# Cross-attention adjacency and a mixture of experts on one core: idle products by a new constant, new orders, and another last step

## The reference

```
# stage 1, for each of 4 batches (4 heads are summed, so Q K^T is one 512x512 product)
sim    = ctx Wq^T (ctx Wk^T)^T * scale           # 512 x 512
A      = sigmoid(sim) where sim is among the 153 largest of its row, else 0
A      = (A + A^T) / 2
x      = x + tanh(g_xattn) * ((1 - gamma) * layernorm(x) + gamma * A)
# stage 2, for each of 2048 tokens
n      = layernorm(x)
best 2 of 8 experts by softmax(n gate_w), their shares normed, times alpha
y_e    = gelu(n fc1[e] + b1[e]) fc2[e] + b2[e]    # 512 -> 512 -> 512
x      = x + tanh(g_ffn) * sum over the two experts of share * y_e
```

## Time and profile before

| what | value |
|---|---|
| median of 3 runs | 366.69 us |
| lowest, highest | 365.43, 367.62 us |
| the profiled execution | 365.13 us |
| its span on the core | 363.4 us |
| mean granted TensorE clock | 0.958 |
| busy PE, PEld | 324.3 us (89%), 232.9 us (64%) |
| busy DVE, ACT, POOL | 200.7 us (55%), 165.0 us (45%), 100.1 us (28%) |
| DMA | 65.79 MB, mean 181 GB/s |

### The profile page before, as it was taken

How to read it: one execution, slowest core, us unless ns; L and a number is a source line. 1 busy time by engine, 2 the same in 40 slices (tenths; PEclk the granted TensorE clock), 3 DMA queues, 4 the chain that set the end, 5 groups by cost and what they waited for, 6 DMA issues and landing times.

```text
span 363.4 us, 6131 instructions
## 1 busy us (share of the span) xinstructions
PE 324.3 (89%) x1937; PEld 232.9 (64%) x1937; DVE 200.7 (55%) x697; ACT 165.0 (45%) x384; POOL 100.1 (28%) x141
## 2 busy tenths in 40 slices
PE   6906899779998999899999989999999999999960
PEld 4402667677764786678778576777785877577610
DVE  0488698887879777898886372636206112311010
ACT  2485515389996746256786222232222213132320
POOL 5001001361111357114307431331733111312031
PEclk9975699899999999999999999999999999999996
DMA  2999989977974696876627587744678854533253
GB/s 91 379 392 369 352 298 331 378 267 139 305 145 123 144 243 231 146 161 183 113 54 181 191 173 135 211 100 81 203 163 149 176 119 104 111 64 87 30 74 46
DMA packets 53636, 65.79 MB, mean 181 GB/s; under 512 B 9792, under 2 KB 28512, under 8 KB 53600
## 3 DMA queue, kind: packets, MB, share of 16 engines
q1 hardware_dynamic: 46144, 47.99, 43.7%
q0 software_dynamic: 7456, 17.37, 24.7%
HBM read 39.56 MB, written 25.78 MB: 180 GB/s over the span
## 4 chain that ended last, share of the span: by engine, by line
PE 50%; issue 18%; DVE 14%; DVEq 5%; DMA 5%; POOL 3%; POOLq 2%; ACT 2%; ACTq 0%
PE ps L1711 21%; PE ps L1684 13%; PE ps L1694 10%; DMA out_rows<-ab,dst 3%; PE ps L1647 2%; POOL xs_rows L566 2%; DMA meta<-xs_rows 2%; DVE top L1087 1%; DVE stats L1012 1%; PE ps L1607 1%; PE ps L1721 1%; PE ps L1627 1%; PE ps L1639 1%; POOLq L530 1%; DVEq L1086 1%
## 5 line engine op out<-in xcount | busy, mean ns | idle before, releaser
L1684 PEld LDWEIGHTS ps<-xgT_r,weights 128*128 128x128 f32 x768 | 87.8, 192 | 8.3 <-issue 6.7
L1684 PE MATMUL ps<-xgT_r,weights 128*128 128x128 f32 x768 | 89.6, 276 | 3.6 <-ACT xgT_r L743 2.0
L1711 PE MATMUL ps<-weights,act_r 128*128 128x512 f32 x192 | 86.3, 595 | 1.5 <-ACT act_r L766 1.5
L580 POOL DMA_INDIRECT out_rows<-ys,dst x24 | 37.9, 1578 | 115.2 <-ACT ys L773 70.0
L1711 PEld LDWEIGHTS ps<-weights,act_r 128*128 128x128 f32 x192 | 34.9, 190 | 38.4 <-issue 36.5
L766 ACT ACTIVATE act_r<-ps,b1T 128x128 f32<-128x128 f32 x96 | 27.1, 365 | 38.9 <-PE ps L1684 38.8
L1694 PEld LDWEIGHTS ps<-sim,weights 128*128 128x128 f32 x256 | 35.2, 190 | 1.9 <-issue 1.7
L566 POOL DMA_INDIRECT xs_rows<-ab,pos x32 | 31.9, 998 | 14.5 <-issue 9.1
L1694 PE MATMUL ps<-sim,weights 128*128 128x160 f32 x256 | 35.6, 299 | 0.0
L773 ACT ACTIVATE ys<-ys,meta 128x512 f32<-128x512 f32 x24 | 17.3, 719 | 31.3 <-DVE ys L1322 31.3
L1322 DVE TENSOR_TENSOR ys<-ps,b_r 128x512 f32<-128x512 f32 x24 | 16.5, 686 | 23.4 <-PE ps L1711 22.0
(11 more groups left out here) (206 smaller groups left out, 419.0 us busy)
## 6 DMA issues: line engine op xcount, KB each, us to landing
weights<-in_L_ffn_fc_w SPq DMA_DIRECT2D x16, 1024.0 KB, 8.0
b_r<-in_L_ffn_fc_b SPq DMA_DIRECT2D x32, 256.0 KB, 4.1
xg_r<-xs_rows SPq DMA_DIRECT2D x88, 64.0 KB
xb<-in_x SPq DMA_DIRECT2D x4, 1024.0 KB, 7.1
out_rows<-xb SPq DMA_DIRECT2D x4, 1024.0 KB, 5.5
sim<-xs_rows SPq DMA_DIRECT2D x32, 80.0 KB
xs_rows<-weights SPq DMA_DIRECT2D x1, 2064.0 KB, 13.5
xs_rows<-weights SPq DMA_DIRECT2D x2, 516.0 KB, 5.9
```

Source lines behind the costliest of these rows:

```text
L580: pool.indirect_dma_start(out=out_rows, out_offset=bass.IndirectOffsetOnAxis(ap=dst[:, k % 2, e:e + 1], axis=0), in_=result_rows(m), in_of ...
L1684: mm = pe.matmul(ps[:, n % 2, i * P:(i + 1) * P], weights[:, e, 0, h, i * P:(i + 1) * P], rows[:, h * P:(h + 1) * P], start=(h == 0), stop ...
L1711: mm = pe.matmul(ps[:, 2 + m % 2, :], rows, weights[:, e, 1, i, :], start=(i == 0), stop=(i == IB - 1))
```

## The change

The idle products read a new constant `warm`, which VectorE fills with ones. TensorE waits for it with `warm_ok` instead of for `consts`, runs 36 idle products instead of 24, and gets two further groups of 8, ahead of `project(0)` and ahead of the first scores. The fill is the first statement of VectorE's list; the wait at the top of VectorE's program (line 978) is untouched and comes before it.

The last part is changed. `tails(1)` comes ahead of expert 7's second layer and takes its number, 32; expert 7's result is now number 33 (`LAST_NO`). Expert 7's second layer is split into two halves around `hand_over` and `merge(1)`. `hand_over` is one product more: a third matrix of zeros and ones picks from the weighed tails those rows whose token is also in expert 7's tile, and brings them to that token's row there. `find_twins` adds up which tail rows were handed over, and these too are pointed at thrown-away rows. So expert 7's tile and the tails have no token in common, and `add_result(3, 7)` no longer waits until the tails have been added: it waits for the add before them. Bias and share of expert 7's tile are applied by two operations of VectorE (`open_last`, `close_last`) in place of `add_bias` and `weigh`.

The lists of all five engines are rearranged. The first part of TensorE's, and the parts of the other lists of which the text speaks, are shown; "..." marks what is left out.

```
-BUSY_LOADS, BUSY_SEARCH, BUSY_MASK = 24, 36, 48
+BUSY_LOADS, BUSY_SEARCH, BUSY_MASK = 36, 36, 48
...
+        warm = sb("warm", [P, P], BF16)
...
+        LAST_NO = FULL + E + GROUPS - 1
+
         def result_no(k, e):
-            return k * E + e if k < BATCH - 1 else FULL + (SHARE + 1) * (e // SHARE) + e % SHARE
+            if k < BATCH - 1:
+                return k * E + e
+            return LAST_NO if e == E - 1 else FULL + (SHARE + 1) * (e // SHARE) + e % SHARE
...
@@ SyncE's list
             store_x1(0)
-            fill_pads()
-            load_weights(6)
             load_x(2)
-            load_weights(7)
             load_meta(0)
             load_rows(0, 2)
             load_rows(0, 3)
+            fill_pads()
             fill_ends()
...
             load_rows(0, 6)
             load_b2(0, 4)
+            load_weights(6)
+            load_rows(0, 7)
             store_x1(1)
             load_b2(0, 5)
-            load_rows(0, 7)
+            load_weights(7)
...
@@ GpSimd, add_result
-                pool.wait_ge(ys_ok, m + 1)
-                if m:
-                    pool.wait_ge(added, 16 * m)
+                if m == LAST_NO:
+                    pool.wait_ge(twins_ok, 1)
+                    pool.wait_ge(last_ok, 1)
+                    pool.wait_ge(added, 16 * (m - 1))
                 else:
-                    pool.wait_ge(pad_out, 32)
+                    pool.wait_ge(ys_ok, m + 1)
...
@@ GpSimd's list
+            scatter_rows(3, 0)
+            scatter_rows(3, 1)
             add_result(2, 3)
-            for t in range(BT):
-                scatter_rows(3, t)
+            scatter_rows(3, 2)
             add_result(2, 4)
+            scatter_rows(3, 3)
             add_result(2, 5)
...
             add_result(3, 6)
+            add_tails(1)
             add_result(3, 7)
-            add_tails(1)
...
@@ ScalarE's list (new order around the first gelu)
             norm_plain(0)
             norm_plain(1)
-            norm_plain(2)
-            norm_plain(3)
             scores(2, 0)
             scores(2, 1)
             leaning(0)
+            norm_plain(2)
+            context(3)
+            norm_plain(3)
+            picked(0)
             scores(2, 2)
             scores(2, 3)
...
+            signs(1, 0)
             query(3)
-            signs(1, 0)
-            picked(0)
             picked(1)
             signs(1, 1)
             gelu(0, 0)
...
@@ VectorE
+            def open_last():
+                u = LAST_NO % 2
+                dve.wait_ge(handed_ps, 1)
+                dve.wait_ge(b2_in_s[u], b2_count(LAST_NO))
+                dve.wait_ge(added, freed(LAST_NO))
+                dve.scalar_tensor_tensor(result_rows(LAST_NO), b2_r[:, u, :], last_share, ps[:, SMALL_BANK, :], ALU.mult,
+                                         ALU.add)
+
+            def close_last():
+                u = LAST_NO % 2
+                dve.drain()
+                dve.wait_ge(y_ps, LAST_NO + 1)
+                dve.scalar_tensor_tensor(result_rows(LAST_NO), ps[:, 2 + u, :], last_share, result_rows(LAST_NO), ALU.mult,
+                                         ALU.add).then_inc(last_ok, 1)
...
@@ VectorE's list
+            dve.memset(warm[:], 1.0).then_inc(warm_ok, 1)
             coefficients()
             x_stats(0, 0)
-            for t in range(BT):
-                sim_stats(0, t)
+            sim_stats(0, 0)
+            x_stats(0, 1)
+            sim_stats(0, 1)
+            sim_stats(0, 2)
+            sim_stats(0, 3)
             first_guess(0)
-            keep_gate_sum()
+            x_stats(0, 2)
             count(0, 0)
-            x_stats(0, 1)
             narrow(0, 0)
             count(0, 1)
-            x_stats(0, 2)
+            x_stats(0, 3)
             narrow(0, 1)
             count(0, 2)
-            x_stats(0, 3)
             x_var(0)
             narrow(0, 2)
+            x_stats(1, 0)
             x_scales(0)
-            x_stats(1, 0)
+            keep_gate_sum()
...
             best_two(0)
+            gaps(0)
             norm(0, 2)
             norm(0, 3)
-            x_var(1)
-            sim_stats(1, 0)
-            gaps(0)
-            sim_stats(1, 1)
             one_hot(0)
             shares(0)
+            places(0)
+            sim_stats(1, 3)
             one_hot(1)
...
@@ TensorE
-                        pe.matmul(ps[:, 3, 0:P], ones_b[:], ones_b[:], start=True, stop=True)
+                        pe.matmul(ps[:, 3, 0:P], warm[:], warm[:], start=True, stop=True)
...
+            def hand_over():
+                pe.wait_ge(tails_w, GROUPS)
+                pe.wait_ge(twins_ok, 1)
+                pe.matmul(ps[:, SMALL_BANK, :], twins[:, GROUPS, :], result_rows(tail_no_of(GROUPS - 1)), start=True,
+                          stop=True).then_inc(handed_ps, 1)
...
@@ TensorE's list
+            pe.wait_ge(warm_ok, 1)
+            keep_busy(BUSY_LOADS)
             pe.wait_ge(consts, 2)
-            keep_busy(BUSY_LOADS)
             pe.wait_ge(qk_in, 32)
             pe.matmul(ps[:, 0, 0:C], wq, wk, start=True, stop=True).then_inc(m_ps, 1)
             turn_context(0)
             pe.wait_ge(m_sb, 1)
+            keep_busy(8)
             project(0)
+            keep_busy(8)
             for t in range(BT):
                 scores(0, t)
+            turn_context(1)
+            project(1)
+            scores(1, 0)
+            scores(1, 1)
             turn_b1()
             sum_gate()
-            turn_context(1)
-            project(1)
+            busy_to_threshold()
+            prove(0)
             turn_context(2)
-            scores(1, 0)
-            scores(1, 1)
-            busy_to_threshold()
             scores(1, 2)
-            prove(0)
             scores(1, 3)
             keep_busy(BUSY_MASK)
...
-            scores(2, 0)
-            scores(2, 1)
+            for t in range(3):
+                scores(2, t)
+            rank(0)
+            scores(2, 3)
             keep_busy(12)
-            rank(0)
-            scores(2, 2)
-            scores(2, 3)
+            project(3)
             pick_rows(0)
-            project(3)
             pick_rows(1)
             layer1(0, 0)
             layer1(0, 1)
             layer2(0, 0)
+            layer2(0, 1)
             layer1(0, 2)
-            layer2(0, 1)
...
+            layer1(1, 7)
             layer2(1, 6)
-            layer1(1, 7)
+            layer2(1, 7)
             adjacency(3, 0)
             adjacency(3, 1)
             layer1(2, 0)
-            layer2(1, 7)
...
             layer2(3, 6)
-            layer2(3, 7)
             tails(1)
+            layer2(3, 7, 0, 2)
+            hand_over()
             merge(1)
+            layer2(3, 7, 2, 4)
```

More of the change, by code:

```diff
@@ L846, in _ @@
                 halve(1, t)
-            weigh(0, 1)
-            gelu(0, 3)
+            signs(2, 0)
             gelu(0, 4)
-            signs(2, 2)
-            for t in range(BT):
-                affine_x(2, t)
+            affine_x(1, 3)
+            signs(2, 1)
             weigh(0, 2)
             turned(1, 0)
+            weigh(0, 3)
             turned(1, 1)
-            weigh(0, 3)
             turned(1, 2)
             turned(1, 3)
-            candidates(2, 0)
-            candidates(2, 1)
+            leaning(1)
@@ L861, in _ @@
             scores(3, 0)
-            candidates(2, 2)
+            gelu(0, 5)
+            signs(2, 2)
+            weigh(0, 4)
+            for t in range(3):
+                candidates(2, t)
+            gelu(0, 6)
+            affine_x(2, 0)
+            candidates(2, 3)
+            squash(2, 0)
             scores(3, 1)
-            candidates(2, 3)
+            weigh(0, 5)
+            affine_x(2, 1)
+            squash(2, 1)
+            gelu(0, 7)
             scores(3, 2)
-            leaning(1)
@@ L894, in _ @@
-            weigh(1, 2)
-            turned(2, 3)
-            for t in range(BT):
-                candidates(3, t)
-            gelu(1, 3)
-            squash(3, 0)
+            turned(2, 3)
+            candidates(3, 1)
+            squash(3, 0)
+            candidates(3, 2)
+            candidates(3, 3)
+            weigh(1, 2)
+            gelu(1, 4)
+            weigh(1, 3)
             squash(3, 1)
+            leaning(2)
+            gelu(1, 5)
+            squash(3, 2)
+            squash(3, 3)
@@ L1358, in _ @@
                 total(0, t)
-            for t in range(BT):
-                add(0, t)
+            add(0, 0)
+            add(0, 1)
+            x_stats(1, 1)
+            add(0, 2)
+            add(0, 3)
             for t in range(BT):
@@ L1464, in _ @@
-            add(2, 3)
-            for t in range(BT):
-                x1_stats(2, t)
-            x1_var_of(2)
-            narrow(3, 1)
-            norm_bias(2)
-            for t in range(BT):
-                norm(2, t)
-            turn_rows(1, 4)
-            add_bias(10)
-            narrow(3, 2)
-            x_scales(3)
-            largest(3, 0)
+            add_bias(10)
```

(16 more changed lines are left out.)

493 lines of the change are left out of this document (268 added, 225 removed).

## The result

The changed kernel takes 379.99 us (median of 3 runs, 378.96 to 380.74), against 366.69 us before. The ratio is 1.0363, interval 1.03 to 1.0427: 13.3 us slower, where 3.4 us faster was forecast. The profiled execution took 378.96 us with a span of 377.1 us, 13.7 us more than the 363.4 of before.

A forecast was written before the change was run, and what follows sets the result against it. Bounds: batch 0's chain before 66.8 us, three engines near their limit to 114, TensorE's own work to 346.8, then a 16.6 us tail. Sum -0.2 + 0 - 3.2 = -3.4 us, so 363.3 us, range 359.9 to 368.2.

The forecast's parts named there:

- The dense stage: TensorE from 114 to 346.8 us: a 1.2 us gain set against new waits, 0 us, bounds -3.0 and +3.0.
- The prediction's own sign of being wrong: Wrong if TensorE waits more than 4 us between batch 1's transposes and the last layer.
- The first idle products: Program start: fill at 9.34 us, products near 9.6, joined matrix at 13.7, 8.7 us later than before.
- the rival had 8.7: Program start: products run from the first microsecond, the 8.7 us are never lost, 354.7 us; chance 0.03.
- What the products give back: First scores and projection: higher clock saves 4.0 us, 2.6 of it on scores; first guess 4.7 us later.
- the rival that the clock gives nothing: First scores and projection: the products don't raise the clock, the 4.0 us stay, 367.3 us; chance 0.13.
- The chain of batch 0: Up to 114 us: `pick_rows(0)` at 69.2, `layer2(0, 0)` 0.7 to 0.8 us later, front -0.2, bounds -2 and +5.
- The rival that ScalarE keeps the front's delay: 66.8 to 114 us: ScalarE has no slack, 4.7 us stand at 114 us, 368.2 us in all; chance 0.14.
- both layers run densely: TensorE behind the start of `layer2(0, 0)`: no gaps, and batch 1's 1.0 us wait for masks goes.
- the forecast of -0.2: The whole front at 114 us: +0.8 - 1.0 = -0.2 us, bounds -2 and +5.
- The tail: Behind 346.8 us: last add issued at 353.1 us instead of 356.37, -3.2 us, bounds -1.2 and -4.0.

The follow-up runs named there:

- e1: The changed kernel with GpSimd's roots free of drains; VectorE adds the constant and GpSimd's power instruction signals itself: 365.52 us, ratio 1.0022.
- e9: e1 with one GpSimd drain put back, between the wait for the variance and the power instruction: 380.78 us, ratio 1.0384.
- e6: e1 with the fill of `warm` put ahead of VectorE's first wait for `consts`: 358.16 us, ratio 0.981.
- e12: e1 without the 36 idle products at the start and the two groups of 8; VectorE's fill stays: 366.99 us, ratio 1.0045.
- e2: The kernel before with the drain edit of e1: 366.19 us, ratio 1.0063.
- e4: The kernel before with the new last part alone, all lists otherwise old: 365.43 us, ratio 1.0041.
- e5: e4 with the load of the tails' b2 rows moved ahead of expert 7's: 362.62 us, ratio 0.9948.
- e3: The changed kernel with `rstd_of_x(3)` and `rstd_of_x1(2)` again ahead of `add_result(1, 1)` in GpSimd's list: 377.59 us, ratio 1.0384.
- e8: The changed kernel with weights 6 and 7 loaded at their old places, ahead of batch 0's rows: 382.13 us, ratio 1.0464.
- e11: e6 with `gelu(0, 0)` ahead of `signs(1, 1)` and `query(0)` ahead of the tanh coefficients on ScalarE: 358.09 us, ratio 0.979.
- e10: The old lists with everything else of e6: new last part, fill first, idle products, no drains around the roots: 362.34 us, ratio 0.992.

## Why the prediction was wrong

**The step that failed** is "The dense stage". It set "0, bounds -3.0 (all idle time) and +3.0", with the ground that new waits on five lists can't be read from the trace, and checked one, the scatters of batch 3. The pause of GpSimd inside `rstd_of_x1` stood in the trace of before, with 3.54 us, and its DMA issue beside it. I had taken no row of it, since it cost nothing there. Two questions would have found it: which engine takes part in the chain x1, norm, gate, `best_two`, `rank`; and what stands ahead of its step in the new list. A part of the answer was visible: for batch 2 the change moves `add_result(1, 1)` ahead of `rstd_of_x1(2)`. The runs put some 13 us in the place of the 0 (after against e1, e9 against e1). The prediction's own sign of being wrong, more than 4 us of TensorE's waits behind batch 1's transposes, is what the trace shows: 14.2 us. Without the drains the stage is within its bounds, at +1.5 us by the traces of before and e1.

The bounds failed for another reason too. +3.0 was the old idle time mirrored, and nothing makes the loss as large as what was left to gain. A wait of TensorE can also cost twice: 4.03 us of idle time brought 2.4 us at a lower clock behind it. Not each does: behind the waits of 3.00 and 1.26 us the granted clock stayed at 1.00.

**The first idle products: right.** The trace after has what the prediction asks for:

```profile
9.39 0.17 DVE L1382 MEMSET warm<- 128x128 bf16 x1 [9.39 <-POOLq L556]
```

```profile
9.68 4.03 PE L1660 MATMUL ps<-warm 128*128 128x128 bf16 x36 [9.68 <-DVE warm L1382]
13.50 0.74 PE L1840 MATMUL ps<-act_r 128*128 128x128 f32 x2
...
17.56 3.86 PE L1685 MATMUL ps<-ctxT,qT 128*128 128x512 f32 x8 [0.23 <-ACT qT L696]
...
69.92 0.61 PE L1744 MATMUL ps<-xg_r,act_r 128*128 128x128 f32 x4
...
86.21 8.83 PE L1789 MATMUL ps<-weights,act_r 128*128 128x512 f32 x16 [1.84 <-ACT act_r L785]
```

Fill at 9.34 predicted and 9.39 found, products 9.6 and 9.68, matrix 13.7 and 13.50. So the change didn't do what its name says, by the wait left in front of the fill; e6 measures what that is worth, 7.4 us of span, where the rival had 8.7. The Trainium skill, "PSUM — Partial Sum Buffer", section "Engine vs sequencer instructions", with its strict FIFO, is borne out by the row of the fill.

**What the products give back: right.** 2.4 us on the scores (6.28 before, 3.86 after), where 2.6 was taken; the rival that the clock gives nothing is out. e12 shows the trade: the 36 products cost 3.9 us and, with the two groups of 8, give back about as much. The reading of the granted clock from 10 to 12 us is 1.00 before and in the changed kernel too, while the durations say half: 0.79 us for a score before, and 0.11 us for an idle product in the 36 at the start, against 0.07 in a group of 48 later. The Trainium skill, "TensorE: Matmul & The Clock Gate", section "What's actually happening", calls the low level the default of an idle array; e12's 6.63 us agree with that.

**The chain of batch 0: right up to `layer2(0, 0)`, short behind it.** `pick_rows(0)` was given 69.2 us and came at 69.92; `layer2(0, 0)` was given 86.5 with 2.9 us of idle time that gelu ends, and came at 86.21 with 1.84. The rival that ScalarE keeps the front's delay is out. But the prediction's "both layers run densely" left out the clock: from 88 to 90 us it reads 0.50, and the two second layers take 8.83 us, where two in a row take 7.03 elsewhere in the kernel. `layer1(0, 5)` stands at 125.65 us against 126.09 of before, which looks like the forecast of -0.2; yet two scores of batch 3, which stood in front of it before, now stand behind. The first place with the same work in front of it is the end of `layer2(0, 7)`: 150.95 us before, 154.83 in the change, of which 3.0 are the wait for `rank`, and 151.94 in e1. So by these traces the front took +1.0 us for a term of -0.2, within its bounds. There was luck in the base as well: the traces of e2, e4 and e5, whose TensorE has the old front too, have `pick_rows(0)` at 63.52, 65.00 and 63.07 us, where the one trace of before has 66.77, and they end `layer2(0, 7)` at 147.5 to 150.6. By them the front costs more, +1.3 to +4.5 us. No run shows why the old front varies so; in the change, e1, e3, e8 and e9, which share its front, `pick_rows(0)` lies between 69.57 and 70.53. e11 shows that moving gelu ahead in ScalarE's list saves the wait and the slow layers, and that other waits take the time back.

**The tail: right.** From the end of `layer2(3, 6)` to the end of the span were 20.0 us before (343.4 to 363.4) and are 17.0 now:

```profile
360.07 3.64 PE L1800 MATMUL ps<-weights,xb 128*32 128x512 f32 x32
...
367.18 1.88 PE L1789 MATMUL ps<-weights,xb 128*128 128x512 f32 x4
...
368.73 1.54 POOL L605 DMA_INDIRECT out_rows<-ab,dst_t  x1 [5.28 <-ACT ab L804]
...
370.62 1.54 POOL L596 DMA_INDIRECT out_rows<-ab,dst  x1 [0.35 <-issue]
```

-3.0 against -3.2 predicted, and the two last adds are issued 1.9 us apart, as said; by whole runs, e5 measures -1.9 us on its own, within the bounds of -1.2 to -4.0 (in e1 the same stretch takes 17.8 us, -2.2). e4 shows a cover the prediction didn't name: the load of the tails' bias had to change places too.

**The account.** In parts of the time before: last part -0.5% (e5); idle products with the fill first, and no drains, -0.3% (e5 to e10, whose intervals overlap); the new orders -1.1% (e10 to e6); fill behind the wait +2.1% (e6 to e1); drains met by the new orders +3.4% (e1 to after). The sum is 3.6%, the result, as it must be: each term is the step from one run to the next. All but the last are 0.2% together, where the forecast had -0.9%. The traces of before and e1, which differ by 0.3 us of span, divide it by the prediction's terms: +1.0 us at the end of `layer2(0, 7)` for -0.2, another +1.5 us from there to the end of `layer2(3, 6)` (345.9 against 343.4 us) for 0, and -2.2 us in the tail for -3.2. Each is the difference of two single executions. The +1.5 us are not more than their spread: that stretch takes 192.4 to 194.0 us in the kernels with the old lists and 193.9 to 195.2 in those with the new ones and no drains. So with the drains away the forecast would still have been some 4 us too low; single traces don't tell how that divides.

## What to carry to other kernels

Find the small steps that every engine gives to the longest chain, and look for pauses in them even where they cost nothing now: what hides them is the order of the lists, and the order is what a change like this one alters. Where GpSimd both issues adding DMAs and computes, keep drains out of its computing steps; let the last instruction's own completion raise the semaphore, and give an operation that needs a drain behind it to another engine. The idle time that is there is no bound on new waits: that is the number of new meetings times their length, plus the clock behind them. To compare two kernels whose lists differ, take a place with the same work in front of it.

## What the runs showed of the hardware

A drain on GpSimd waited until the indirect adding DMA that GpSimd had issued before it had landed. In three kernels (before, after, e9) seven idle times in front of the power end 0.2 to 0.8 us behind the landing of such a DMA, which came 4.8 to 9.2 us behind its issue; without the drain the next instruction ran 1.0 us behind the issue (e1). Two shorter pauses at a drain are less clear: 1.47 us in batch 3 before, which ended 1.4 us behind a landing, and 1.36 us in e3, when no add was on its way. So a pause of that size at a drain isn't shown to be an add's. The time to landing of one such add moved between 4.7 and 10.2 us, so such a drain has no fixed price.
